# Cross attention of a decoder layer: VectorE and ScalarE work ordered by a quad's two steps

## The reference, cut to what matters

```python
k = (key @ Wk.T + bk).reshape(b, lk, HEADS, HEAD_DIM)
v = (value @ Wv.T + bv).reshape(b, lk, HEADS, HEAD_DIM)
scores = jnp.einsum('bqhd,bkhd->bhqk', q * scale, k)
probs = jax.nn.softmax(scores, axis=-1)
attn = jnp.einsum('bhqk,bkhd->bqhd', probs, v)
```

## Time and profile before

| What | Value |
|---|---|
| median of three runs | 2379.48 us |
| profiled execution: its own time, its span | 2381.39 us, 2379.6 us |
| TensorE busy | 2330.8 us (98%) |
| VectorE, ScalarE, GpSimd busy | 1510.4 (63%), 1347.2 (57%), 1399.3 us (59%) |
| mean granted TensorE clock | 0.993 |
| cross attention with its full pace | about 540 to 1840 us of the span |

### The profile page before, as it was taken

The page is one execution under the profiler, slowest core; times in us unless marked ns, Lnnn a source line. Parts: engine busy times, 40 slices in busy tenths (PEclk is TensorE's granted clock), DMA queues, the critical chain, the costliest instruction groups (busy, mean ns, idle before and its releaser), DMA issues.

```text
span 2379.6 us, 58683 instructions
## 1 busy us (share of the span) xinstructions
PE 2330.8 (98%) x21642; PEld 2033.3 (85%) x21642; DVE 1510.4 (63%) x2563; ACT 1347.2 (57%) x3322; POOL 1399.3 (59%) x1211
## 2 busy tenths in 40 slices
PE   8999989999999999999999999999999899999999
PEld 7888758988888888888888888888888699998998
DVE  4676788836767677676767677676766734435342
ACT  5888852236666666666666666666666642231321
POOL 4777677347667667667666667667665533333332
PEclk9999979999999999999999999999999999999999
DMA  7444478537777777777677777777677831101000
GB/s 190 131 130 120 118 205 321 212 100 195 185 198 199 204 188 203 192 200 208 178 207 193 198 197 197 196 197 204 179 201 198 253 133 36 50 18 66 7 33 24
DMA packets 254825, 384.60 MB, mean 162 GB/s; under 512 B 116760, under 2 KB 132184, under 8 KB 254552
## 3 DMA queue, kind: packets, MB, share of 16 engines
q1 hardware_dynamic: 229976, 330.65, 49.4%
q10 hardware_dynamic: 24576, 50.36, 8.3%
HBM read 126.33 MB, written 40.60 MB: 70 GB/s over the span
## 4 chain that ended last, share of the span: by engine, by line
PE 75%; DVE 1%; issue 1%; ACT 1%; ACTq 0%; POOL 0%; DVEq 0%; POOLq 0%
PE D_ps_p L69 42%; PE D_ps_s L1995 7%; PE D_ps_p L2022 6%; PE E_ps_g L69 6%; PE E_ps_u L69 6%; PE E_ps_d L69 5%; PE E_ps_y L69 3%; ACT D_e L1650 1%; DVE D_columns L1792 0%; PE E_ps_t L2051 0%; ACTq L1666 0%; DVE D_turned L1806 0%; DVE E_stats_a L1849 0%; DVE E_r_a L1865 0%; ACT D_values L1639 0%
## 5 line engine op out<-in xcount | busy, mean ns | idle before, releaser
L1511 POOL TENSOR_SCALAR D_e<-D_e,D_columns 128x722 f32<-128x722 f32 x256 | 538.5, 2103 | 438.1 <-DVE D_columns L1798 437.8
L1792 DVE TENSOR_REDUCE D_columns<-D_ps_s 128x1 f32<-128x723 f32 x512 | 439.7, 899 | 350.2 <-PE D_ps_s L1995 350.0
L1650 ACT ACTIVATE D_e<-D_ps_s,D_columns 128x723 f32<-128x723 f32 x512 | 436.9, 861 | 238.5 <-DVE D_columns L1792 238.5
L1806 DVE STREAM_TRANSPOSE D_turned<-D_e 128x768 f32<-128x768 f32 x512 | 495.5, 972 | 21.1 <-DMA D_pT<-D_turned 20.3
L69 PE MATMUL D_ps_p<-D_ctx_high,cross_wk_high 128*128 128x384 f32 (+1 forms) x1024 | 346.0, 338 | 2.9 <-DVEq L1818 1.5
L69 PE MATMUL D_ps_p<-D_ctx_low,cross_wk_high 128*128 128x384 f32 (+1 forms) x1024 | 333.2, 325 | 0.0
L69 PE MATMUL D_ps_p<-D_ctx_high,cross_wk_low 128*128 128x384 f32 (+1 forms) x1024 | 333.0, 325 | 0.0
L1657 ACT ACTIVATE D_e<-D_e,D_columns 128x722 f32<-128x722 f32 x256 | 230.2, 899 | 59.8 <-DVE D_columns L1798 59.8
L69 PE MATMUL D_ps_p<-cross_wv_high,D_ctx_low 128*128 128x512 f32 (+1 forms) x656 | 257.9, 393 | 0.0
L69 PE MATMUL D_ps_p<-cross_wv_low,D_ctx_high 128*128 128x512 f32 (+1 forms) x656 | 257.7, 393 | 0.0
L69 PE MATMUL D_ps_p<-cross_wv_high,D_ctx_high 128*128 128x512 f32 (+1 forms) x656 | 255.8, 390 | 0.7 <-ACT D_values L1639 0.7
(11 more groups left out here) (264 smaller groups left out, 5225.6 us busy)
## 6 DMA issues: line engine op xcount, KB each, us to landing
D_pT<-D_turned SPq DMA_DIRECT2D x1536, 96.0 KB, 2.7
D_pT<-D_turned ACTq DMA_DIRECT2D x512, 96.0 KB, 2.9
D_craw<-in_ctxT SPq DMA_DIRECT2D x124, 361.0 KB, 4.2
self_v<-wstage SPq DMA_DIRECT2D x25, 256.0 KB, 2.6
A_v<-self_v SPq DMA_DIRECT2D x32, 200.0 KB
self_o<-A_o SPq DMA_DIRECT2D x32, 200.0 KB, 4.1
x<-C_x SPq DMA_DIRECT2D x5, 1280.0 KB, 5.8
cross_q<-C_qo SPq DMA_DIRECT2D x20, 320.0 KB, 4.1
```

Source lines behind the costliest of these rows:

```text
L1511: pool.tensor_scalar(head, head, inv[:, 2 * (s % 2):2 * (s % 2) + 1], None, ALU.mult)\
L1650: act.activation(e[n // 2 % 2][:, n % 2, 0:PARTS * PART].rearrange("p (a c) -> p a c", a=PARTS), parts_of(n), ACT.Exp, bias=neg_max[:, n % ...
L1792: dve.tensor_reduce(neg_max[:, n % 4:n % 4 + 1], parts_of(n), AX.XY, ALU.max, negate=True)\
L1806: dve.transpose(turned[quad % 2][:, :, 2 * (s % 2) + h, :].rearrange("p j (t r) -> p t j r", r=32), e[s % 2][:, h, :].rearrange("p (t j r) ...
```

## The change

The main loops of ScalarE and VectorE run by quads in place of steps. VectorE does two maxima, the result, two more maxima, the inverses of both steps, and then all four turns of this same quad. The turns of a quad's second step, which stood in the next quad behind its first maxima, now stand ahead of them. ScalarE does the four exponentials with the key takes after the second and the fourth of them, then both normalisations, the value take, and the four diagonal moves of the quad before in a row. At the end of the loop the conversion of the output weights (`low_wo`, `first_highs`, `last_first_low`) keeps its order but stands at other places. TensorE, GpSimd and SyncE keep their programs.

```diff
--- before.py
+++ after.py
@@ -1741,8 +1741,25 @@
                     act.wait_ge(sem_loaded, USED_ONCE + 16)
                     act.activation(target[0][:, k, :], source[:, k, :], ACT.Copy).then_inc(sem_high, 1)
 
-                for s in range(FIRST, MAIN):
-                    step(s)
+                def pair_of_steps(s):
+                    take_units("v", s - 1)
+                    if s >= 0:
+                        exps(2 * s)
+                        exps(2 * s + 1)
+                    take_units("k", s)
+                    if s >= 0:
+                        exps(2 * s + 2)
+                        exps(2 * s + 3)
+                    take_units("k", s + 1)
+                    if s >= 0:
+                        normalise_second(s)
+                        normalise_second(s + 1)
+                    take_units("v", s)
+                    if s > 1:
+                        move_diagonal(s)
+                        move_diagonal(s + 1)
+
+                def first_highs(s):
                     if MAIN - 6 < s < MAIN - 1:
                         for k in range(2):
                             n = 2 * (s - MAIN + 5) + k
@@ -1750,6 +1767,11 @@
                                 high_of(wos, wo_raw, wo_loaded[n // 2], n, wo_high)
                             else:
                                 high_of(acts, acts_raw, first_loaded[(n - KD) // 2], n - KD, o_high)
+
+                for s in range(FIRST, MAIN, 2):
+                    pair_of_steps(s)
+                    first_highs(s)
+                    first_highs(s + 1)
                 step(MAIN)
                 step(MAIN + 1)
 
@@ -1831,7 +1853,7 @@
                     if s in sum_at:
                         take_result(sum_at[s])
                     for h in range(2):
-                        if 0 < s <= STEPS:
+                        if MAIN < s <= STEPS:
                             turn_blocks(s - 1, h)
                         if s < STEPS:
                             inverse(2 * s + h)
@@ -1924,13 +1946,27 @@
                     dve.tensor_tensor(acts[1][:, KD - 1, :], acts_raw[:, KD - 1, :], acts[0][:, KD - 1, :].bitcast(F32),
                                       ALU.subtract).then_inc(o_low, 1)
 
-                for s in range(MAIN + 1):
-                    step(s)
-                    if MAIN - 3 <= s < MAIN - 1:
+                def pair_of_steps(s):
+                    maxima(s)
+                    if s in sum_at:
+                        take_result(sum_at[s])
+                    maxima(s + 1)
+                    inverse(2 * s)
+                    inverse(2 * s + 1)
+                    if s >= MAIN - 4:
                         for k in range(2):
-                            low_wo(2 * (s - MAIN + 3) + k)
-                    if s == MAIN - 1:
-                        last_first_low()
+                            low_wo(s - MAIN + 4 + k)
+                    inverse(2 * s + 2)
+                    inverse(2 * s + 3)
+                    turn_blocks(s, 0)
+                    turn_blocks(s, 1)
+                    turn_blocks(s + 1, 0)
+                    turn_blocks(s + 1, 1)
+
+                for s in range(0, MAIN, 2):
+                    pair_of_steps(s)
+                last_first_low()
+                step(MAIN)
                 maxima(MAIN + 1)
                 second_sum(0, 0)
                 rest_of_step(MAIN + 1)
```

## The result

The changed kernel takes 2519.82 us (median of four runs, 2519.10 to 2522.80) against 2380.0 us for the kernel before in the same session: 1.0585 times, 95% interval 1.0562 to 1.0608. The forecast was 2512 us, slower. The profiled execution has a span of 2517.3 us, 137.7 more than before.

A forecast was written before the change was run, and what follows sets the result against it. TensorE was taken as the bound. The profiled 2381.4 us plus 122 for 61 late places and 10 for tails made 2513.4; less 1.9 against the median, about 2512 us, range 2475 to 2575.

The forecast's parts named there:

- Points 1 to 3: At steps 4, 5 of 8: inverse 0.73 us later, GpSimd's normalisations still 4.86 us apart, VectorE's next maxima 3.07 us late.
- Point 4: TensorE behind the late maxima: second key unit 1.90 us late, value unit 2.1 us; the next, long quad catches up.
- Points 5 and 6: Steps 0, 1 of 8 lose 1.9 us too; 61 places at 2.0 us make 122 us.
- Point 7: Seven batches with tail splits between GpSimd's normalisations: about 1.5 us each, 10 us.
- Points 8 and 9: ScalarE's later key take and four moves in a row, SyncE's moves behind the fourth turn: no cost; ScalarE's uncovered, 30 us.
- Point 10: End of the loop with the moved conversions: taken as zero, up to 5 us gained or lost.
- A (absorbed): GpSimd ends its second normalisation some 2 us sooner and slack swallows the delay: no change, 2379 us; chance 0.06.
- B: Issue of ScalarE's four moves holds up exponentials and takes in every quad: 2640 us, at half 2576; chance 0.06.
- D (faster): TensorE's holes before scores, 38.9 us, come from the last exponential's late release and are won back: 2342 us; chance 0.04.
- C, the clock: New 1.9 us pauses drop the clock to half, 1.7 us each, 104 us at all 61 places: 2616 us; chance 0.04.

The follow-up runs named there:

- The piece schedules: The change with GpSimd's context piece after step 4 moved behind step 5: 2445.1 us; with the one after step 8 also moved behind step 7: 2394.3 us.
- the dose: The change with GpSimd's piece after steps 4 and 8 made longer, its rounding copy done twice: 2593.2 and 5839 us; run once more, 2591.3 us.
- moves apart: The change with two of ScalarE's four diagonal moves put back between the two normalisations: 2518.1 us (1.0571 against the kernel before).
- experiment 3: The change with both GpSimd normalisations of a quad together, its copies, pieces and tail splits behind them: 2387.0 us (1.0015 against the kernel before).
- experiment 7: The change, GpSimd's normalisations first, its last low parts behind them, ScalarE's rounding of the last two chunks one quad earlier: 2384.1 us (1.0012 against the kernel before).
- turns back (experiment 2): The change with the second step's turns back in the next quad, behind its first maxima and result: 2443.2 us (1.0251 against the kernel before).
- VectorE's order alone: VectorE's order of the change with ScalarE's old order: 2533.0 us (1.0628 against the kernel before).
- ScalarE's order alone: ScalarE's order of the change with VectorE's old order: 2612.8 us (1.0963 against the kernel before).

## Why the prediction was right, and where it was off

**What bounds the kernel.** Right. With the order of the change and nothing in its way the loop takes 1337.6 us, as before; nothing was to be gained there.

**Points 1 to 3, the chain.** Right to a tenth of a microsecond. Counted from the scores of the quad, the inverse was forecast at 5.07 and came at 5.08; the first normalisation 5.31 and 5.33; the gap to the second 4.86 and 4.86; the first turn 12.36 and 12.32; the next maxima 14.14 and 14.09.

**Point 4.** The second key unit was forecast 1.90 us late and is 1.74 late (6.55 against 4.81 us from its scores); the value unit 2.1 forecast, 2.0 measured. The 0.15 us between 1.90 and 1.74 are two releases (0.03 us into the first turn and 0.05 behind the result, put at about 0.1 each) and the two maxima (1.61 us, put at 1.65). The quads between the late ones kept their time, as stated.

**Points 5 and 6.** 61 places at 2.0 us were 122 us; the 45 that could be measured by themselves give 1.97 each, 120.0 for 61. The piece schedules show both places apart, and the dose shows that GpSimd's time there is paid nearly in full (0.82 of 0.88).

**Point 7.** 10 us, measured 8.6, but the agreement is in part luck: three of the loop's falls of the clock lie in these batches, at 1.3 us each, and point 7 had no clock in it. Without them the tails cost 4.7 us, 0.7 in place of 1.5 in each of seven.

**Points 8 and 9.** Right: moves apart changed nothing, and with the same programs of ScalarE, VectorE and SyncE experiment 3 lost nothing in the loop. But "no cost" for ScalarE's order holds only beside VectorE's new order; alone it made the slowest kernel. The prediction never asked this of it.

**Point 10.** This term was off in size. The end of the loop was put at zero, between -5 and +5; it is +5.6. The last low part of the first outputs (L1946) comes late. Who waited, 1975 to 2015 us, and the clock behind these waits by the windows view:

```profile
PE E_ps_y L69 <- DVE E_acts_low L1946: 3.8, 1, 3.8
PE D_ps_p L2058 <- ACT D_values L1639: 2.4, 1, 2.4
...
1994.30:2001.10 6.80, 4.33 (x10) 3.46 (x11) 5.33 (x9) 2.49 (x5) 6.25 (x5) 0.50 0.20 52
```

Between the scores of quads 125 and 127 TensorE's holes sum to 7.9 us beside 4.3 before, so 3.6 of the 5.6 us are longer waits. The other 2.0 us are about what the clock costs: it is at half while TensorE works from 1996.8 to 2001.1, and half of 4.3 us is 2.2. I put the late low part down to GpSimd's low parts, which stand between its last two normalisations, and to VectorE's, which stands behind all turns; experiment 7 moved GpSimd's and an earlier step of ScalarE together, so which of them counts was not shown.

The first four quads were not costed either: 4.2 us beyond their regular holes, two falls of the clock among them. Together with point 10 that is 9.8 us, more than the 7.8 that the forecast lacks; the regular places and the tails came out 3.4 us cheaper than forecast.

**The rivals.** A (absorbed) fell: its condition, GpSimd's second normalisation some 2 us sooner, is what experiment 3 made, and there it came true. B fell with the moves apart. D (faster) fell: TensorE's "issue" idle time before scores is 39.1 us over 111 quads in the new trace (600 to 1900 us), as before. C, the clock, was given one of the smallest chances and is true in small part, in other places than it named. In the loop of the kernel before the clock never fell; in the change it fell in seven stretches between 520 and 2030 us, 27 us in sum, five of them (17 us) between the scores of quads 0 and 125. None followed one of the regular pauses of 1.5 to 2.0 us; all seven followed pauses of 2.57 to 4.07 us (start to start of matmuls), in the first four quads, in batches with tails and at the end, which the prediction did not have. Where one falls into a batch with tails, the quad reads 4.26 us more than before in place of 2.97, so 1.3 us each; some 7 us in the loop, not 104.

## What to carry to other kernels

Before grouping waits on an in-order engine, look at what the engine that they wait for does in between, in its own program: two instructions of which the second waits for work behind a 2.8 us filler must not stand ahead of the next stage's first step. The slack of the bound engine (here 1.3 us to its next bank) is the number to compare with, and it is read from the timeline. If an order is wanted for its own sake, move the filler first; here that took one edit and gave back all of the 132.8 us that the loop had lost.

## What the runs showed of the hardware

**The clock fell behind single pauses from 2.1 us on, with TensorE busy most of the time around them.** I had argued from a stretch with TensorE busy 3.31 of 7.10 us. In the kernel with the longer piece TensorE was busy 31.93 of 36.70 us in the stretch before a fall (above). Counted from the first scores to 40 us behind the last ones, with a pause from start to start of matmuls:

| Kernel | pauses 1.5 to 2.0 us | 2.0 to 2.5 | 2.5 to 3.0 | over 3.0 | falls |
|---|---|---|---|---|---|
| before | 3 | 0 | 1 | 0 | 0 |
| turns back (experiment 2) | 10 | 1 | 2 | 0 | 1 |
| the change | 46 | 0 | 10 | 2 | 7 |
| VectorE's order alone | 46 | 8 | 1 | 3 | 8 |
| longer piece | 2 | 1 | 45 | 10 | 22 |
| ScalarE's order alone | 4 | 1 | 35 | 23 | 33 |

Of the pauses of 1.5 us and more, the last one ahead of a fall was at least 2.13 us long in every case. An example from ScalarE's order alone, the pause and then the fall from 2.4 to 1.2 GHz; the third line is the middle of its loop, with a mean clock of 0.96:

```profile
985.00:989.00 4.00, 1.74 (x23) 1.52 (x13) 2.66 (x6) 2.31 (x6) 0.38 (x1) 1.00 0.82 214
989.03:992.45 3.42, 3.42 (x13) 3.42 (x13) 3.10 (x6) 2.00 (x6) 3.33 (x4) 0.51 0.76 172
650.00:1800.00 1150.00, 1023.66 (x10414) 880.16 (x10413) 694.46 (x1193) 652.42 (x1252) 663.95 (x504) 0.96 0.64 168
```

The rule of the Trainium skill (TensorE: Matmul & The Clock Gate, section "HAM oscillation — how this bites in real kernels"), that a loop whose matmuls wait in each pass can drop in each pass, comes closer than I had it: not in each pass, but behind about four to six of ten pauses where they are near 3 us. In the kernel with the longer piece the clock added some 20 us to the 49 us of the piece itself.

**GpSimd's normalisation takes 3.08 us in place of 2.10 when it begins during a subtraction of VectorE, and 2.10 when the subtraction begins later.** At the end of the loop `low_wo` (two subtractions, 1.27 us together) overlaps a normalisation both before and in the change. GpSimd and VectorE in the kernel before:

```profile
1847.29 2.10 POOL L1511 TENSOR_SCALAR D_e<-D_e,D_columns 128x722 f32<-128x722 f32 x1 [2.90 <-DVE D_columns L1798]
1848.06 1.27 DVE L1919 TENSOR_TENSOR E_wo_low<-E_wo_raw,E_wo_high 128x512 fp32r<-128x512 f32 x2
```

In the change (the first row is two normalisations, of 3.08 and 2.10 us), and the durations of all normalisations there, in ns:

```profile
1974.47 5.15 POOL L1511 TENSOR_SCALAR D_e<-D_e,D_columns 128x722 f32<-128x722 f32 x2 [7.23 <-DVE D_columns L1820]
1974.39 1.27 DVE L1941 TENSOR_TENSOR E_wo_low<-E_wo_raw,E_wo_high 128x512 fp32r<-128x512 f32 x2
...
1977.59 1.84 DVE L1828 STREAM_TRANSPOSE D_turned<-D_e 128x768 f32<-128x768 f32 x2 [0.95 <-POOL D_e L1511]
```

```profile
L1511 POOL TENSOR_SCALAR D_e<-D_e,D_columns x256: 2097/2106/3078, 513.3 to 2018.1; 128x722 f32<-128x722 f32 x128
```

Before, the subtractions begin 0.77 us into the normalisation and lie inside it, and it takes 2.10 us. In the change they begin 0.08 us ahead of it, and it takes 3.08. The traces of the experiments say the same: all 19 normalisations that began 0.07 to 0.12 us into such a pair took 3.04 to 3.09 us, one that began 0.03 us ahead of the pair took 2.60, and five in which a subtraction began 0.27 to 0.77 us later took 2.10 to 2.11. The Trainium skill (GPSIMD Engine Reference, section "1. Specifications") names contention of the SBUF interfaces shared with VectorE for VectorE's instructions with two SBUF inputs; the traces agree where the subtraction began first, and show none where the normalisation was well under way. No run here moved `low_wo` alone, so this is read from traces and was not tested.
